# The filter stage's ten edge columns, dealt out for each orientation in runs of lines

## The reference, cut to what matters

```python
def _L3_conv_ref(x):                       # x is group-normalised, [16, 32, 64, 64]
    lstd = ...                             # local standard deviation over 3x3, scaled to 0..1 per channel
    center_k, surround_k = _make_kernels() # 8 orientations each, 21 x 21, sigma (3.65, 3.65/8) and three times that
    tidx = jnp.arange(B) % N_THETAS        # sample b has orientation b mod 8
    center_resp = _per_sample_conv(avg_resp, center_k[tidx])
    surround_resp = _per_sample_conv(avg_resp, surround_k[tidx])
    return jnp.maximum(center_resp - lstd * surround_resp, 0.0)
x = x + _L3_conv_ref(_gn(x))
```

## Time and profile before

| what | us |
|---|---|
| median of 3 runs | 1197.33 |
| lowest, highest | 1196.41, 1201.05 |
| the profiled execution's own time | 1200.27 |
| its span in the trace | 1197.3 |
| PE busy | 1076.6 |
| DVE, ACT, POOL busy | 808.9, 537.1, 321.8 |
| mean granted TensorE clock | 0.961 of full |

### The profile page before, as it was taken

One profiled execution on the slowest core, in us unless ns is written; L12 is line 12 of the kernel. 1 busy time (PEld: TensorE's weight loads), 2 busy tenths in 40 slices (PEclk: granted clock), 3 DMA queues, 4 the chain that ended last, 5 costly groups with the idle time before them and its releaser, 6 DMA issues.

```text
span 1197.3 us, 38501 instructions
## 1 busy us (share of the span) xinstructions
PE 1076.6 (90%) x17036; PEld 790.9 (66%) x17036; DVE 808.9 (68%) x1001; ACT 537.1 (45%) x747; POOL 321.8 (27%) x364
## 2 busy tenths in 40 slices
PE   2999999999999999999923589978989999999997
PEld 2999989999899999999821245433334444444443
DVE  6456585684857848477296978689989645466444
ACT  3524635546364563625334967677941212121110
POOL 1374545535464363545410000022300000000000
PEclk9999999999999999999956988989989999999999
DMA  6020020200202000010001444322354654566551
GB/s 210 7 77 3 3 76 3 76 3 3 76 3 76 3 18 27 3 42 3 3 1 37 105 104 112 91 59 71 93 140 124 190 171 117 171 178 187 152 139 43
DMA packets 52115, 89.77 MB, mean 75 GB/s; under 512 B 8795, under 2 KB 36699, under 8 KB 50940
## 3 DMA queue, kind: packets, MB, share of 16 engines
q1 hardware_dynamic: 44264, 80.56, 24.3%
q10 hardware_dynamic: 7700, 6.89, 2.0%
HBM read 36.89 MB, written 11.99 MB: 41 GB/s over the span
## 4 chain that ended last, share of the span: by engine, by line
PE 74%; DVE 17%; ACT 3%; issue 3%; DMA 2%; SPq 1%; DVEq 0%; ACTq 0%
PE psum L1519 38%; PE psum L1753 16%; PE psum L1764 10%; PE psum L1653 5%; DVE small L711 2%; PE psum L1555 2%; DMA arena<-arena 2%; DVE arena L1008 1%; DVE small L586 1%; DVE X L904 1%; PE psum L1568 1%; DVE arena L1027 1%; DVE arena L1015 1%; PE psum L1541 1%; DVE arena L1021 1%
## 5 line engine op out<-in xcount | busy, mean ns | idle before, releaser
L1519 PE MATMUL psum<-arena 128*128 128x64 f16 (+2 forms) x11904 | 514.9, 207 | 22.3 <-DMA arena<-arena 12.6
L1519 PEld LDWEIGHTS psum<-arena 128*128 128x128 f16 x11904 | 497.8, 99 | 38.2 <-issue 12.7
L625 DVE TENSOR_TENSOR arena<-psum,arena 128x512 f32<-128x512 f32 x128 | 87.9, 691 | 170.0 <-PE psum L1519 142.4
L1753 PE MATMUL psum<-arena 128*128 128x512 f16 (+2 forms) x936 | 192.4, 366 | 0.0
L1753 PEld LDWEIGHTS psum<-arena 128*128 128x128 f16 x936 | 92.2, 99 | 98.7 <-issue 3.3
L1431 POOL TENSOR_SCALAR arena<-arena,constants_f 128x256 f16<-128x256 f16 x126 | 138.6, 1128 | 0.0
L1427 POOL TENSOR_TENSOR arena<-arena 128x256 f16<-128x256 f32 x63 | 51.7, 820 | 309.5 <-ACT arena L1189 309.5
L1184 ACT ACTIVATE arena<-arena 128x256 f16<-128x256 f32 x63 | 26.5, 420 | 208.4 <-issue 105.5
L1764 PE MATMUL psum<-arena 120*128 120x512 f16 (+1 forms) x528 | 116.9, 379 | 0.0
L1764 PEld LDWEIGHTS psum<-arena 120*128 120x128 f16 (+1 forms) x528 | 51.4, 97 | 61.8
L1475 POOL TENSOR_TENSOR arena<-arena 128x1024 f32<-128x1024 f32 x16 | 30.4, 1899 | 206.8 <-ACT arena L1331 153.9
(11 more groups left out here) (209 smaller groups left out, 1413.3 us busy)
## 6 DMA issues: line engine op xcount, KB each, us to landing
arena<-in_filter_tables SPq DMA_DIRECT2D x8, 1280.0 KB, 8.6
arena<-arena SPq DMA_DIRECT2D x32, 264.0 KB, 3.9
X<-in_x SPq DMA_DIRECT2D x16, 512.0 KB, 4.7
arena<-arena SPq DMA_DIRECT2D x32, 256.0 KB, 4.0
out<-X SPq DMA_DIRECT2D x16, 512.0 KB, 4.0
arena<-edge_columns SPq DMA_DIRECT2D x90, 80.0 KB
arena<-edge_columns ACTq DMA_DIRECT2D x70, 80.0 KB
arena<-arena SPq DMA_DIRECT2D x32, 140.0 KB, 2.5
```

Source lines behind the costliest of these rows:

```text
L625: v.tensor_tensor(out_, bank_rows(k), biasrow, ALU.add).then_inc([g.staged0, g.staged1][k], 1)
L1519: last = mm(conv[k][:, c0:c1], win[:, kk, lx, y + e, dx:dx + W, :].rearrange("p w s -> p (w s)"), wt[:, lw, d, w0:w1], start=(n == 0), sto ...
L1753: mm(bank[4 * s + 2 * f + hf][:, C * lo:C * hi], tb[:, f, d + 2, lt], xt[s][:, hf, lx, YP + d + lo:YP + d + hi].rearrange("p y c -> p (y c)"),
```

## The change

The 240 places of each half are no longer cut in two at fixed rows. For each orientation a hand-written list deals them out into a near and a far slice (112 to 128 places each), so that the narrow filter touches the near slice alone: its far window (7 and 9) has an all-zero table at every t and is left out. In `rest_of` each sample so has six products fewer. The lists are runs of lines in the scratch tensor; for t = 0, 1 and 7 the lines there are ordered by column instead of by row. A run is one transfer, and a list entry with four numbers behind the block is a small rectangle of lines, again one transfer.

Transfers for one half of one sample, by orientation t = 0 to 7: 7 each before; now 14, 13, 20, 10, 9, 10, 20, 13. The lines are 240 in each case. Both Fori loops of SP's and ACT's filter stage become straight code. Diff, cut:

```diff
-NREAL = 12 * NBW
+BY_COLUMN = (0, 1, 7)
+EDGE_NEAR = {
+    0: ((1, 0, 20), (2, 0, 20), (3, 0, 20), (4, 0, 20), (5, 0, 20), (0, 2, 2, 0, 5), (6, 0, 2, 0, 5)),
+    1: ((1, 0, 8), (2, 0, 12), (3, 0, 20), (4, 0, 28), (5, 0, 30), (6, 0, 2, 0, 7)),
+    2: ((2, 10, 1), (2, 20, 2), (2, 30, 3), (3, 0, 4), (3, 10, 5), (3, 20, 6), (3, 30, 7), (4, 0, 40), (5, 0, 40), (6, 0, 20)),
+    3: ((2, 20, 15), (3, 0, 40), (4, 0, 40), (5, 0, 30)),
+    4: ((2, 10, 30), (3, 0, 40), (4, 0, 40), (5, 0, 10)),
+}
+EDGE_FAR = {
+    0: ((1, 20, 20), (2, 20, 20), (3, 20, 20), (4, 20, 20), (5, 20, 20), (0, 2, 2, 5, 5), (6, 0, 2, 5, 5)),
+    1: ((0, 2, 2, 0, 10), (1, 8, 32), (2, 12, 28), (3, 20, 20), (4, 28, 12), (5, 30, 10), (6, 0, 2, 7, 3)),
+    2: ((0, 20, 20), (1, 0, 40), (2, 0, 10), (2, 11, 9), (2, 22, 8), (2, 33, 7), (3, 4, 6), (3, 15, 5), (3, 26, 4),
+        (3, 37, 3)),
+    3: ((0, 20, 20), (1, 0, 40), (2, 0, 20), (2, 35, 5), (5, 30, 10), (6, 0, 20)),
+    4: ((0, 20, 20), (1, 0, 40), (2, 0, 10), (5, 10, 30), (6, 0, 20)),
+}
+def edge_line(t, row, column):
+    row = G - 1 - row if t > NT // 2 else row
+    return G * column + row if t in BY_COLUMN else NBW * row + column
+        def edge_pieces(t, s, h):
+            line = 2 * YN * C
+            for k, part in enumerate(edge_parts(t, h)):
+                at_ = 0
+                for a, lines in part:
+                    n = sum(len(run) for run in lines)
+                    src = edge_dram[s, h, lines[0][0]:lines[0][-1] + 1, :, C * a:C * (a + NY)]
+                    if len(lines) > 1:
+                        src = bass.AP(edge_dram.tensor, src.offset,
+                                      [[G * line, len(lines)], [line, len(lines[0])], [YN * C, 2], [1, C * NY]])
+                    yield edges[s][at_:at_ + n, k, h], src
+                    at_ += n
@@ store_edges
-                        sp.dma_start(edge_dram[s, h, NBW * r:NBW * r + NBW],
+                        first, last = edge_line(t, r, 0), edge_line(t, r, NBW - 1)
+                        sp.dma_start(edge_dram[s, h, first:last + 1:(last - first) // (NBW - 1)],
@@ load_edges (and load_right on ACT in the same way)
-                    for part, at_, r0, n, a in ((0, 0, 0, 4, 1), (0, 4, 0, 4, 2), (0, 8, 0, 4, 3),
-                                                (1, 0, 0, 4, 4), (1, 4, 0, 4, 5), (1, 8, 0, 2, 6), (1, 10, 2, 2, 0)):
-                        sp.dma_start(edges[s][NBW * at_:NBW * (at_ + n), part, h],
-                                     edge_dram[s, h, NBW * r0:NBW * (r0 + n), :, C * a:C * (a + NY)]
-                                     ).then_inc((edge_in if h == 0 else right_in)[s], 16)
+                    for dst, src in edge_pieces(t, s, h):
+                        sp.dma_start(dst, src).then_inc((edge_in if h == 0 else right_in)[s], 16)
@@ rest_of
-                    for window, src in ((5, outer[s][:, hf]), (6 + 2 * hf, edges[s][0:NREAL, 0, hf]),
-                                        (7 + 2 * hf, edges[s][0:NREAL, 1, hf])):
-                        if not filled[t, f, window]:
-                            continue
+                    near, far = (edge_count(part) for part in edge_parts(t, hf))
+                    used = [v for v in (5, 6 + 2 * hf, 7 + 2 * hf) if filled[t, f, v]]
+                    for window in used:
+                        rows = {5: P, 6 + 2 * hf: near, 7 + 2 * hf: far}[window]
@@ filters
-                pe.wait_ge([g.edge_in0, g.edge_in1][s], 16 * 7 * (t + 1))
-                pe.wait_ge([g.right_in0, g.right_in1][s], 16 * 7 * (t + 1))
+                pe.wait_ge([g.edge_in0, g.edge_in1][s], edge_loads(t, 0))
+                pe.wait_ge([g.right_in0, g.right_in1][s], edge_loads(t, 1))
```

More of the change, by code:

```diff
@@ L50, with edge_parts, edge_count, edge_rows @@
 NPS = 3
-NREAL = 12 * NBW
 KB, KQ, KV, KK = range(4)
 NSIDE, NCENT = 256, 640
+BY_COLUMN = (0, 1, 7)
+EDGE_NEAR = {
[5 rows of a table added]
+}
+EDGE_FAR = {
[6 rows of a table added]
+}
+def edge_line(t, row, column):
+    row = G - 1 - row if t > NT // 2 else row
+    return G * column + row if t in BY_COLUMN else NBW * row + column
+def edge_parts(t, hf):
+    parts = []
+    for part in (EDGE_NEAR[min(t, NT - t)], EDGE_FAR[min(t, NT - t)]):
+        pieces = []
+        for a, *of in part:
+            if len(of) == 2:
+                lines = [range(of[0], of[0] + of[1])]
+                if hf:
+                    lines = [range(40 - of[0] - of[1], 40 - of[0])]
+            else:
+                r0, c0 = of[0], of[2]
+                if hf:
+                    r0, c0 = G - of[0] - of[1], NBW - of[2] - of[3]
+                lines = [range(G * c + r0, G * c + r0 + of[1]) for c in range(c0, c0 + of[3])]
+            pieces.append((6 - a if (t > NT // 2) != (hf == 1) else a, lines))
+        parts.append(pieces)
+    return parts
+def edge_count(part):
+    return sum(len(run) for a, lines in part for run in lines)
+def edge_rows(t, part):
+    place = {edge_line(t, q, c): (q, c) for q in range(G) for c in range(NBW)}
+    at = [(4 * (a - 3) + place[n][0], place[n][1]) for a, lines in part for run in lines for n in run]
+    return np.array(at).T
 def host_constants():
@@ L72, in host_constants @@
     r, w = p // NH, p % NH
-    j, wi = p // NBW, p % NBW
-    real = p < 12 * NBW
     rows_in, cols_in, used = [], [], []
@@ L78, in host_constants @@
     rows_in.append(np.where(r < 2, 12 + r, r - 12)), cols_in.append(w), used.append(p >= 0)
[L79 to L85, removed]
     tab = np.zeros((NT, P, 2, NWIN, 2, P), np.float16)
@@ L90, in host_constants @@
         yr = -xx * np.sin(th) + yy * np.cos(th)
+        del rows_in[6:], cols_in[6:], used[6:]
+        for hf in range(2):
+            for part in edge_parts(t, hf):
+                rows, cols = edge_rows(t, part)
+                unused = np.zeros(P - len(rows), int)
+                rows_in.append(np.concatenate([rows, unused]))
+                cols_in.append(np.concatenate([cols, unused]) + (NH if hf == 0 else -NBW))
+                used.append(p < len(rows))
         for cs, m in enumerate((1.0, 3.0)):
@@ L385, in win3, with edge_loads @@
             return 0 <= tap <= 2
+        def edge_pieces(t, s, h):
[10 more added lines that the diff above has]
+                    at_ += n
+        def edge_loads(t, h):
+            return 16 * sum(len(part) for turn in range(t + 1) for part in edge_parts(turn, h))
         @block.sync
@@ L543, in _ @@
             load_tables(1, 1)
[L545 to L551, removed]
+            for t in range(NT - 2):
+                for s in range(2):
+                    prefetch(t + 1, s)
+                    store_out(t, s)
+                load_tables(t + 2, t % 2)
             for s in range(2):
@@ L1366, in load_right @@
                 a.wait_ge([g.edge_out0, g.edge_out1][s], 128 * (t + 1))
[L1367 to L1371, removed]
+                for dst, src in edge_pieces(t, s, 1):
+                    a.dma_start(dst, src).then_inc([g.right_in0, g.right_in1][s], 16)
             a.wait_ge(g.zero3, 1)
@@ L1396, in _ @@
             root(0, 0)
-            with a.Fori(0, NT - 2) as t:
+            for t in range(NT - 2):
                 high(t + 1, 0)
@@ L1757, in rest_of @@
                 def rest_of(f, hf):
-                    for window, src in ((5, outer[s][:, hf]), (6 + 2 * hf, edges[s][0:NREAL, 0, hf]),
-                                        (7 + 2 * hf, edges[s][0:NREAL, 1, hf])):
-                        if not filled[t, f, window]:
-                            continue
+                    near, far = (edge_count(part) for part in edge_parts(t, hf))
+                    used = [v for v in (5, 6 + 2 * hf, 7 + 2 * hf) if filled[t, f, v]]
+                    for window in used:
+                        rows = {5: P, 6 + 2 * hf: near, 7 + 2 * hf: far}[window]
+                        src = outer[s][:, hf] if window == 5 else edges[s][0:rows, (window - 6) % 2, hf]
                         for lt, lx in ((0, 0), (0, 1), (1, 0)):
-                            rows = src.shape[0]
                             last = mm(bank[4 * s + 2 * f + hf], tb[0:rows, f, window, lt], src[:, lx],
-                                      start=False, stop=(window == 7 + 2 * hf and lt == 1), skip_group_check=True)
+                                      start=False, stop=(window == used[-1] and lt == 1), skip_group_check=True)
                     return last
```

## The result

The changed kernel takes 1247.04 us (median of 4, 1243.51 to 1252.11) against 1198.51 us for the kernel before (median of 4): a ratio of 1.0432, 95% interval 1.0386 to 1.0479, so +48.5 us. The forecast was 1239 and +42. The profiled execution is the slowest of its four, 1252.11 us with a span of 1250.3.

The account below looks back on a forecast made before the run. The prediction took PE to bound the filter stage, with added load issues on SP's and ACT's queues making it wait. Stalls 46.5 plus clock 15.8 minus gain 20.8 gave +42 us, 1239; own range 1229 to 1249, 8 in 10 1214 to 1260.

Parts of the forecast that it names:

- the stalls: PE's waits for edge loads in the filter stage, summed over the samples by the recurrence: 46.5 us lost.
- The gain: Filter stage, PE: six products fewer for each of 16 samples, 96 x 0.216 = 20.8 us saved if PE stays the bound.
- The price of an issue: SP's and ACT's queues: each edge load costs about 0.78 us, 0.84 with the step on SP, whatever its size.
- rival of cheap small pieces: Loads under ten lines at t = 2 and 6 cost 0.33 us instead of 0.78: +16, 1213 us; chance 0.11.
- that of dear rectangles: Dearer pieces: rectangles at 1.08 us instead of 0.84 give +50; with dearer loads generally, 1247 to 1278 us; chance 0.09.
- Samples 0 and 1: Orientation 0: SP issues 28 loads instead of 14 per sample, so PE stalls 10.6 and 7.6 us before the rest.
- the recurrence: Filter stage, sample by sample: queue issues, landings and PE's readiness give each stall; PE ends at 1233 against 1191.3 us.
- The sentence of the Trainium skill: Initiating a DMA is usually small beside the DMA, so added issues cost nothing: 20.8 us gain; prediction rejected it.
- The landing: Edge loads: the last piece lands 1.2 us after its issue ended, from a 62 KB transfer landing 2.0 us after issue.
- Samples 4, 5, 12, 13: t = 2 and 6, 20 loads for each sample: PE stalls 8.3, 3.2, 6.6 and 3.2 us before the rest.
- Sample 15: Last sample: no stall listed; the recurrence takes 12.0 us of PE to the rest, then 30 products.
- The clock: PE after each stall over 2.5 us: slower products cost 2.25 us, seven times, 15.8 us in all.

Follow-up runs that it names:

- the run with seven loads: Changed kernel's products and straight code, but the seven transfers for a half of the kernel before: 1174.12 us, ratio 0.9837 against the kernel before.
- The split to ACT's queue: Changed kernel, but at orientation 0 ACT's queue issues the right half's 14 loads of each of the two samples: 1226.76 us, ratio 1.0288 against the kernel before.
- small tables: Changed kernel with the table loads of orientations 2 to 7 cut from 1280 KB to 32 KB each: 1234.37 us, ratio 1.0321 against the kernel before.
- the interleaved kernel: Changed kernel with each block's high and low part side by side, a line being one run of 2048 bytes: 1175.89 us, ratio 0.9836 against the kernel before.
- the kernel with merged transfers: Changed kernel with equal runs of several blocks as one transfer, t = 2 and 6 keeping 36 products: 1280.40 us, ratio 1.0711 against the kernel before.

## Why the prediction was right

It was right in direction and cause, and the size was within the range: +42 against +48.5 us. The size owes something to luck. The sum was made for the stage of a profiled execution, and there 41.5 us stand against 55.1 measured, 13.6 too few; in the medians, for the reasons above, 6.5 too few. The mis-sized term is the stalls, 46.5 us forecast and 56.1 measured, and inside it misses of both signs partly cancel. By its steps:

- **The gain**, 96 products, 20.8 us if PE waits for nothing. Right: 20.7 us of busy time in the run with seven loads, ratio 0.9837.
- **The price of an issue**, 0.78 us whatever the size, 0.84 with the step. Right: medians of 0.794 and 0.790, 28 issues in 23.3 us for a forecast of 23.5. The rival of cheap small pieces fell with the minimum of 0.63 us and with 0.81 us each at t = 2, and that of dear rectangles as well: 28 issues with eight of them took 23.3 us (25.4 at 1.08 for each), 13 with three of them 11.0. (The prediction counts a rectangle at t = 4; the list there has none, and the sum doesn't change by it. It looked for DMA and SP's queue in the chain; ACT's queue has the larger share there.)
- **Samples 0 and 1**: waits of 10.6 and 7.6 forecast, 11.07 and 8.71 measured. The split to ACT's queue took 17 us away and the return of orientation 0 to its old form 19, by the ratios, as the recurrence's start says.
- **The sentence of the Trainium skill** (DMA: Bandwidth & Descriptors, Issuing engines are not separate DMA queues) that the time to initiate a DMA is usually small relative to the DMA itself is no guide here. The rows and the split decide: 28 issues last 23.3 us, and the same transfers from a second queue are worth 17 us.
- **The landing**, 1.2 us behind the last issue, read off another kind of transfer (arena to arena). It was mis-sized. It is 1.4 to 1.7 where nothing large goes out before the last load, and 2.6 at sample 15, where SP sent two outputs of 512 KB beside it. But behind samples 3, 7, 9 and 11 the next tables leave SP while ACT's last load is still being issued (at 7 and 11 PE comes so late that it waits under 1 us). Sample 3: tables out at 976.50, ACT's loads issued until 977.23, PE released at 984.13. At samples 5 and 13 the tables left 0.3 and 0.1 us behind ACT's last issue, and PE was released 1.6 and 1.5 us behind it. I had forecast no wait at sample 3, 1.8 at 9; it was 5.0 and 5.6. With small tables both are nearly gone (0.56 and none), and the whole effect of the tables, the delay of the stores that the forecast did have included, is 13 us.
- **Samples 4, 5, 12, 13** (t = 2 and 6): 8.3, 3.2, 6.6, 3.2 forecast, 1.2, 5.2, 5.1, 3.4 measured. Sample 4 waits less because PE arrived later, having waited at sample 3: both wait for the same chain, so I had the total better than the places.
- **Sample 15**: no wait forecast, 5.2 us measured, and 6.5 with small tables. ACT's loads ended at 1226.29 and PE was released at 1228.84. The step that failed is the 12.0 us of PE ahead of the rest. Both kernels work the last sample half by half: 30 products of `rows_of` for the left half, then the wait for all edge columns, the right half's too, then 15 of the rest (x30 and x15 in the rows above). So PE was ready at 1223.6; behind 60 products it would have come at 1229.4, after the release.

```python
                if last_sample:
                    rest_of(0, 0)
                    rest_of(1, 0).then_inc(g.filtered, 1)
                    rows_of(0, 1)
                    rows_of(1, 1)
```

- **The clock**, seven falls of 2.25 us, 15.8. Measured 17.1 us of slower products behind nine waits, 1.4 to 2.8 each. The granted clock falls behind waits as forecast.
- **Samples without a wait**: 6, 7 and 11 nearly so (0, 0.9, 0.4 us), 3 not.

## What to carry to other kernels

A product left out is worth its time only while everything it waits for is early; before adding transfers to a queue, multiply their number by the issue time of their own form and lay it beside the slack, which here was 2 us for 12 us of added issues. Look at the form before the number: making each line one contiguous run cut the issue from 0.79 to 0.33 us and turned a loss of 4% into a gain of 1.6%. Fewer transfers are no aim in themselves: merged with a small outer dimension they cost more here than the many plain ones. And look where a work order changes at its end: the last sample, dealt in halves, comes early for its loads, and waits there for a half that it doesn't need yet.

## What the runs showed of the hardware that was not expected

- An edge load with two runs of 1024 bytes for each partition costs its queue 0.79 us to issue, one with a single run of 1024 or of 2048 bytes 0.33 us, whether it has few lines or 40. Rectangles keep a higher price: 28 loads of orientation 0, eight of them rectangles, took 14.3 us in the interleaved kernel, the rectangles 0.73 to 0.91 us each.
- In the kernel with merged transfers, whose sources have an outer dimension of 2, 3 or 5 and up to 120 lines, single issues lasted up to 7.2 us, and a 512 KB store landed after 10.6 us instead of 4.0. Which of the two does it is open.
- Loads on ACT's queue land up to 6.9 us behind the last issue when SP sends 1280 KB 0.5 to 0.7 us before the end of that issue: issued until 977.23, there at 984.13. Where the 1280 KB went out 0.1 to 0.3 us behind the last issue it was 1.5 to 1.6. Why is not shown.
- After waits of 11.1 and 8.7 us PE's next 30 products took 8.0 and 9.0 us instead of 6.65, with the granted clock at 0.73 over the stretch from 905 to 921 us.
